# Rebuilding the last stage of an encoder, cross-attention and expert kernel

## The reference, cut to what matters

```python
x1 = x @ sw1.T + sb1;  x2 = x @ sw2.T + sb2
shared_out = ln(silu(x1) * x2, g, b) @ sw3.T + sb3         # all 2048 tokens
x_moe = x[index_b, index_t]                                # 512 chosen tokens
shared_scores = sigmoid(x_moe @ sg_w.T + sg_b)
expert_scores = sigmoid(x_moe @ eg_w.T + eg_b)
top1_idx = argmax(expert_scores + exp_bias)
shared_w, expert_w = softmax([shared_scores, top1_score])
h1 = x_moe @ ew1.T + eb1;  h2 = x_moe @ ew2.T + eb2        # per expert
z = ln(silu(h1) * h2, g', b')
expert_out = (z @ ew3.T + eb3)[top1_idx]
final_out = shared_out.at[index_b, index_t].set(shared_out * shared_w + expert_out * expert_w)
```

## Time and profile before

| | us |
|---|---|
| median of 3 runs | 835.39 (835.33 to 836.73) |
| the profiled execution | 835.16 |
| its span, first to last instruction | 833.4 |
| PE busy | 723.0 (87%) |
| DVE busy | 650.1 (78%) |
| POOL busy | 379.1 (45%) |
| ACT busy | 337.4 (40%) |

### The profile page before, as it was taken

How to read it: one execution, slowest core, us unless ns; L and a number is a source line. 1 busy time by engine, 2 the same in 40 slices (tenths; PEclk the granted TensorE clock), 3 DMA queues, 4 the chain that set the end, 5 groups by cost and what they waited for, 6 DMA issues and landing times.

```text
span 833.4 us, 29134 instructions
## 1 busy us (share of the span) xinstructions
PE 723.0 (87%) x10978; PEld 571.7 (69%) x10978; DVE 650.1 (78%) x1858; ACT 337.4 (40%) x710; POOL 379.1 (45%) x647
## 2 busy tenths in 40 slices
PE   4788469999999999999999999998889888734895
PEld 3567447888888888888888888876556656412673
DVE  4786556787878788887877888789999999845965
ACT  4656224444343444434343444434445545412200
POOL 2788712435353454535444453543345345254132
PEclk9766589999999999999999999999999999955797
DMA  7776300000000000000000000002221222122000
GB/s 272 244 238 226 140 2 2 4 2 4 2 3 3 2 4 3 3 3 3 3 4 3 3 4 9 9 22 73 91 89 60 78 90 80 32 86 75 5 1 6
DMA packets 24655, 41.24 MB, mean 49 GB/s; under 512 B 3727, under 2 KB 16665, under 8 KB 24267
## 3 DMA queue, kind: packets, MB, share of 16 engines
q1 hardware_dynamic: 23096, 37.39, 13.6%
q0 software_dynamic: 704, 1.71, 0.8%
q10 hardware_dynamic: 726, 0.30, 0.1%
HBM read 30.86 MB, written 8.91 MB: 48 GB/s over the span
## 4 chain that ended last, share of the span: by engine, by line
PE 69%; DVE 17%; POOL 5%; issue 5%; ACT 4%; DMA 1%; POOLq 0%; ACTq 0%; DVEq 0%; SPq 0%
PE ps L480 7%; PE ps L474 7%; PE ps L482 6%; PE ps L481 6%; PE ps L684 6%; PE ps L666 5%; DVE mx L1403 5%; PE ps L616 4%; PE ps L722 3%; PE ps L724 3%; PE ps L723 3%; PE ps L618 3%; PE ps L617 3%; PE ps L608 2%; POOL w_lo L1826 2%
## 5 line engine op out<-in xcount | busy, mean ns | idle before, releaser
L1040 ACT ACTIVATE pT<-ps 128x1024 f32<-128x1024 f32 x96 | 93.1, 1022 | 124.5 <-PE ps L666 124.5
L1799 POOL TENSOR_TENSOR rs<-mv,cst 128x1 f32<-128x1 f32 x132 | 31.2, 236 | 178.6 <-DVE mv L1174 140.9
L1403 DVE TENSOR_REDUCE mx<-ps 128x16 f32<-128x2048 f32 x48 | 109.4, 2280 | 1.0 <-PE ps L639 1.0
L1887 POOL TENSOR_TENSOR y<-y,vec 128x256 f32<-128x256 f32 x32 | 23.2, 726 | 170.7 <-DVE y L1177 170.7
L722 PE MATMUL ps<-xh,w_hi 128*128 128x128 bf16 x512 | 99.4, 219 | 0.0
L723 PE MATMUL ps<-xl,w_hi 128*128 128x128 bf16 x512 | 99.3, 219 | 0.0
L724 PE MATMUL ps<-xh,w_lo 128*128 128x128 bf16 x512 | 99.3, 219 | 0.0
L1801 POOL TENSOR_TENSOR rs<-rs,cst 128x1 f32<-128x1 f32 x132 | 73.2, 554 | 10.3
L480 PE MATMUL ps<-w_hi,hh 128*128 x256 | 69.8, 273 | 0.0
L481 PE MATMUL ps<-w_hi,hl 128*128 x256 | 69.8, 273 | 0.0
L482 PE MATMUL ps<-w_lo,hh 128*128 x256 | 69.8, 273 | 0.0
(11 more groups left out here) (366 smaller groups left out, 2495.1 us busy)
## 6 DMA issues: line engine op xcount, KB each, us to landing
stage<-in_w SPq DMA_DIRECT2D x32, 384.0 KB, 3.7
vec<-in_vec SPq DMA_DIRECT2D x4, 896.0 KB, 5.8
vec<-in_tw SPq DMA_DIRECT2D x12, 256.0 KB, 2.8
ctxc<-in_ctx SPq DMA_DIRECT2D x19, 128.0 KB, 2.2
comb<-x SPq DMA_DIRECT2D x16, 128.0 KB, 1.7
comb<-t SPq DMA_DIRECT2D x16, 128.0 KB, 1.8
shared<-x1b SPq DMA_DIRECT2D x16, 128.0 KB, 1.7
out<-x SPq DMA_DIRECT2D x16, 128.0 KB, 1.8
```

The lines of the kernel that those rows point to most:

```text
L1040: A(pT[:, 8 * a:8 * a + 8, :].rearrange("p h q -> p (h q)"), ps[:, 2 * a:2 * a + 2, :].rearrange("p g k -> p (g k)"), ACT.Exp, scale=SCALE ...
L1403: nc.vector.tensor_reduce(mx[:, :], att.rearrange("p g s k -> p (g s) k"), AX.X, ALU.max, negate=True).then_inc(m_max, 1)
```

## The change

The index arithmetic of DVE (`token_rows`) runs once, before DVE's first unit. The keys along the free axis aren't computed any more: PE multiplies each tile's key column, broadcast over 128 columns, by the identity in fp32, so that a PSUM bank holds all 512 keys on every partition; DVE scans that bank four times right after its block 17. PE, ACT and DVE leave their block loops after b = B + 1; what blocks 18 and 19 held of the shared layer stands between steps of the last stage. POOL's gather of the tokens moves from its block 16 to its block 18; the gathers of the shared output are issued two and two behind the second and the third tile's gamma and beta. The expert layers' steps have a new order, with PSUM banks and buffers of their own. Both silus use tanh: x (1 + tanh(x/2)) / 2, in one fused DVE operation, the half being taken up in the gate product.

```diff
@@ sync
-            sp.dma_start(row_i[:, 0, :], ibr_d.broadcast_to([128, M])).then_inc(row_in, 16)
-            sp.dma_start(row_i[:, 1, :], itr_d.broadcast_to([128, M])).then_inc(row_in, 16)
...
+                if b == B:
+                    sp.wait_ge(oT_psum, UNITS + B)
+                    sp.dma_start(tb, tb_d).then_inc(tb_in, 16)
                 put_shared(b - 4)
...
-            sp.wait_ge(oT_psum, UNITS + B)
-            sp.dma_start(tb, tb_d).then_inc(tb_in, 16)
@@ tensor
-            for b in range(1, B + 4):
+            for b in range(1, B + 2):
                 block_c(b, b % 2, ex_of(UNITS - 1)[0] if b == 1 else None)
-            pe.wait_ge(tw_lo, TCHUNKS)
-            pe.wait_ge(tw_hi, TCHUNKS)
+
+            pe.wait_ge(d_gidx, 1)
+            pe.wait_ge(pT_b, UNITS + B)
+            for t in range(MT):
+                last = mm(ps[:, 0, 128 * t:128 * t + 128], ids[:, 4, t:t + 1].broadcast_to([128, 128]), ident,
+                          start=True, stop=True)
+            last.then_inc(d_keys, 1)
...
+            sh_out(B - 2, B - 1)
             pe.wait_ge(tg_split, 1)
...
+            sh_z(B - 1)
             pe.wait_ge(d_sel, D1)
...
-            for step, t in ((choice, 0), (choice, 1), (chosen_hidden, 0), (choice, 2), (chosen_hidden, 1), (choice, 3),
-                            (chosen_z, 0), (chosen_hidden, 2), (chosen_out, 0), (chosen_z, 1), (chosen_hidden, 3),
-                            (chosen_out, 1), (chosen_z, 2), (chosen_out, 2), (chosen_z, 3), (chosen_out, 3)):
+            choice(0)
+            choice(1)
+            chosen_hidden(0)
+            sh_out(B - 1, B - 1)
+            for step, t in ((choice, 2), (chosen_hidden, 1), (choice, 3), (chosen_hidden, 2), (chosen_z, 0),
+                            (chosen_hidden, 3), (chosen_z, 1), (chosen_out, 0), (chosen_z, 2), (chosen_out, 1),
+                            (chosen_z, 3), (chosen_out, 2), (chosen_out, 3)):
                 step(t)
@@ scalar
-                A(sde[:, 0:HM], h[:, 0:HM], ACT.Exp, scale=-1.0).then_inc(s_e, 1)
+                A(sde[:, 0:HM], h[:, 0:HM], ACT.Tanh, scale=0.5).then_inc(s_e, 1)
...
+            sh_zhi(B - 1)
             act.wait_ge(d_oT, D1)
@@ vector
-                ts(sde[:, HM:2 * HM], sde[:, 0:HM], 1.0, None, ALU.add).then_inc(s_e1, 1)
-                dve.wait_ge(s_e1, b + A1)
-                nc.vector.reciprocal(sde[:, 0:HM], sde[:, HM:2 * HM]).then_inc(s_r, 1)
-                dve.wait_ge(s_r, b + A1)
-                tt(h[:, 2 * HM:3 * HM], h[:, 0:HM], sde[:, 0:HM], ALU.mult).then_inc(s_a, 1)
+                stt(h[:, 2 * HM:3 * HM], sde[:, 0:HM], 1.0, h[:, 0:HM], ALU.add, ALU.mult).then_inc(s_a, 1)
...
+            token_rows()
             dve.wait_ge(g_words, 1)
             words_dve.append(word_of(dve, 0))
...
+            for b in range(1, B + 2):
                 block_c(b, b % 2)
+
+            dve.wait_ge(row_in, 16)
+            dve.wait_ge(d_keys, 2)
+            for t in range(MT):
+                last_of_equal(t)
...
+            sh_gnorm(B - 1)
+            sh_sum(B - 2)
...
+            sh_zlow(B - 1)
...
+            mask_tokens(0)
+            mask_tokens(1)
+            sh_sum(B - 1)
+            stored_rows()
+            for step_of, t in ((mask_tokens, 2), (gated, 0), (gated_norm, 0), (mask_tokens, 3), (gated, 1), (mask_z, 0),
+                               (gated_norm, 1), (gated, 2), (mask_z, 1), (gated_norm, 2), (gated, 3), (mask_z, 2),
+                               (gated_norm, 3), (final, 0), (mask_z, 3), (final, 1), (final, 2), (final, 3)):
                 step_of(t)
@@ gpsimd
-                block_c(b, b % 2, ..., gather_tokens if b == B else None)
-            pool.wait_ge(s_shared, 16 * (B + 1))
-            gather(2 * D, 3 * D, shared_d, d_gshared)
+                block_c(b, b % 2, ..., gather_tokens if b == B + 2 else None)
...
+                if t in (1, 2):
+                    pool.wait_ge(s_shared, 16 * (B + 1))
+                    gather(2 * D, 3 * D, shared_d, d_gshared, (2 * t - 2, 2 * t - 1))
```

More of the change, by code:

```diff
@@ L125, in encoder_kernel @@
 def encoder_kernel(nc, x_d, ctx_d, mask_d, maskt_d, w_d, wc_d, vec_d, vc_d, b1_d, gw_d, gb_d, sw_d, sv_d, tw_d, tvec_d, tg_d, tb_d,
-                   ib_d, it_d, ibr_d, itr_d, cst_d, kst_d, pos_d, out, comb_d, shared_d):
+                   ib_d, it_d, cst_d, kst_d, pos_d, out, comb_d, shared_d):
     f32, bf16, i32 = mybir.dt.float32, mybir.dt.bfloat16, mybir.dt.int32
@@ L225, in encoder_kernel @@
         comb = vec[:, R_COMB:R_COMB + MT * 3 * D]
-        rows = w_lo[:, W_ALL - 16 * M:].bitcast(f32).rearrange("p (k m) -> p k m", m=M)
-        row_i, row_f, pos = rows[:, 0:2, :].bitcast(i32), rows[:, 2:4, :], rows[:, 4, :]
-        row_tmp, row_flat, row_key = rows[:, 5, :], rows[:, 6, :], rows[:, 7, :]
+        rows = w_lo[:, W_ALL - 4 * M:].bitcast(f32).rearrange("p (k m) -> p k m", m=M)
+        pos, row_tmp = rows[:, 0, :], rows[:, 1, :]
         finD = vec[:, R_FIN:R_FIN + MT * D]
@@ L289, in encoder_kernel @@
             l2_stats, y2_ready, x_acc)
+        d_keys = g_prod
         A1, D1 = B + 1, UNITS + 1
@@ L893, in _ @@
             pe.wait_ge(tb_in, 16)
+            pe.wait_ge(tw_lo, TCHUNKS)
+            pe.wait_ge(tw_hi, TCHUNKS)
             def choice(t):
@@ L899, in choice @@
                 for e in range(EM):
-                    last = mm(ps[:, 6 + e // 4, 128 * (e % 4):128 * (e % 4) + 128],
+                    last = mm(ps[:, 2 + e // 4, 128 * (e % 4):128 * (e % 4) + 128],
                               identb[0:EM, e:e + 1].broadcast_to([EM, 128]), ohTb[:, 128 * t:128 * t + 128],
@@ L926, in chosen_out @@
                 pe.wait_ge(d_zm, D1 + t)
+                if t == 0:
+                    pe.wait_ge(d_ohb, D1 + MT - 1)
                 if t >= 2:
@@ L1633, in _ @@
             dve.wait_ge(vec_in, 16 * E)
[L1634 to L1644, removed]
             links = [0]
@@ L1673, in rows_of, with token_rows, last_of_equal, stored_rows @@
                 i_link(tt(key, key, flat, ALU.add))
[L1675 to L1679, removed]
+            def token_rows():
+                dve.wait_ge(idx_in, 32)
+                rows_of(idx_i[:, 0, :], idx_i[:, 1, :], ids[:, 0, :], ids[:, 1, :], ids[:, 2, :], ids[:, 3, :], ids[:, 4, :])
+                i_link(cp(gidx[:, :], ids[:, 3, :]))
+                nc.vector.memset(junk[:, 2:3], 0.0).then_inc(d_gidx, 1)
+            def last_of_equal(t):
+                i_link(stt(row_tmp, ps[:, 0, :], ids[:, 4, t:t + 1], pos, ALU.is_equal, ALU.mult))
+                i_link(nc.vector.tensor_reduce(ids[:, 5, t:t + 1], row_tmp, AX.X, ALU.max))
+            def stored_rows():
+                i_link(tt(ids[:, 6, :], ids[:, 5, :], cst[:, C_M:C_M + MT], ALU.is_gt))
+                i_link(ts(ids[:, 7, :], ids[:, 6, :], float(4 * B * S), None, ALU.mult))
+                i_link(tt(ids[:, 8, :], ids[:, 7, :], ids[:, 4, :], ALU.add))
+                i_link(cp(sidx[:, :], ids[:, 8, :]))
+                nc.vector.memset(junk[:, 0:1], 0.0).then_inc(d_sidx, 1)
+            token_rows()
+            dve.wait_ge(g_words, 1)
+            words_dve.append(word_of(dve, 0))
+            for n in range(-1, UNITS + 1):
+                if n == UNITS - 1:
+                    dve.wait_ge(vc_in, 16)
+                block(n, n % 2, vc[:, VC_V:VC_V + D] if causal(n + 1) else bias_of(n + 1), (n - 4) // 2, stats_of(n + 3),
+                      norm_of(n + 2))
+            y_of(at(3), B + 3, UNITS)
+            dve.wait_ge(sv_in, 32)
+            for b in range(1, B + 2):
                 block_c(b, b % 2)
+            dve.wait_ge(row_in, 16)
+            dve.wait_ge(d_keys, 2)
+            for t in range(MT):
+                last_of_equal(t)
             dve.wait_ge(tvec_in, 16)
@@ L1733, in gated @@
                 dve.wait_ge(d_e, D1 + t)
[L1734 to L1738, removed]
+                link(stt(hD[:, 0:HM], de[:, HM * (t % 2):HM * (t % 2) + HM], 1.0, h12[:, 0:HM], ALU.add, ALU.mult))
+                link(stt(hD[:, 2 * HM:3 * HM], hD[:, 0:HM], 0.5, h12[:, HM:2 * HM], ALU.mult, ALU.mult))
+                link(nc.vector.bn_stats(st[:, 2, :], hD[:, 2 * HM:3 * HM]))
                 nc.vector.bn_aggr(mv[:, 2, :], st[:, 2, :]).then_inc(d_var, 1)
@@ L1753, in final @@
             def final(t):
-                shared = (t2, acc)[t % 2]
+                shared = (t2, sum_odd)[t % 2]
                 if t == 0:
@@ L1959, in _, with gather @@
             y_root(B + 3)
-            def gather(c0, c1, rows_d, done):
-                for t in range(MT):
+            def gather(c0, c1, rows_d, done, tiles=range(MT)):
+                for t in tiles:
                     nc.gpsimd.indirect_dma_start(out=comb[:, t * 3 * D + c0:t * 3 * D + c1], out_offset=None,
```

21 lines of the change are left out of this document (13 added, 8 removed).

## The result

The changed kernel took 837.25 us (median, 836.77 to 839.42) against 835.62 before in the same runs: ratio 1.0022, 95% interval 1.0012 to 1.0032. It is slightly slower; forecast was 821.3. The profiled execution took 837.31 us, its span is 835.5.

A forecast was written before the change was run, and what follows sets the result against it. Attention blocks up to 724 us were taken as a ring of PE and DVE, then one chain of small steps over four engines. -6.8 - 7.9 - 1.35 + 2.2 = -13.85 from 835.16 gave 821.3 us, range 815.5 to 828.5.

The forecast's parts named there:

- Part 1: Shared layer's silu by tanh: about 1.1 us less DVE work a block turns idle; value 0, bounds 0 and 16.
- Rival (C): Attention blocks: shorter silu saves 1.1 us in each of 11 blocks, 12 less, 809 us; chance 0.07.
- Part 2: Index arithmetic moved to DVE's start: costs 2.2 us there (bounds 0.6 and 4.3), wins 1.2 in the tail.
- Part 3: Token gathers behind the last shared pieces: first choice product 6.8 us earlier, the 1.2 of Part 2 included.
- Part 4: Expert layers: PE stays fed over the hidden products, output products have half the matmuls, one new wait; -7.9 us.
- Part 5: Scatters at the end: only one issue and its landing, 2.95 us, remain after the last sum; -1.35 us.
- Rival (A): ACT tables: tanh outside exp's set, two loads per shared piece and hidden product; +36, 857 us; chance 0.05.
- Rival (B): Last stage late again: delayed gathers, dearer start, output products at 1.2 GHz, a buffer wait; 828.4 us; chance 0.20.
- (D): No slow clock at the end and a start of +0.6: 817.7 us; chance counted within the forecast's 0.66.

The follow-up runs named there:

- e2: Changed kernel with the index arithmetic back ahead of DVE's block 15: 833.6 us, ratio 0.9970 to the kernel before.
- e10: Kernel before with only the index arithmetic moved to DVE's start: 840.8 us, ratio 1.0049 to the kernel before.
- e8: e6 with the index arithmetic behind DVE's first unit and the token gathers back in POOL's block 16: 821.7 us, against 814.6 with the gathers late.
- e4: Kernel before with only the shared layer's silu by tanh in one fused operation: 849.7 us, ratio 1.0162 to the kernel before.
- e6: Changed kernel with DVE's gate product behind the maxima, their split and the low part of the output: 821.6 us, ratio 0.9834 to the kernel before.
- e5: Changed kernel with POOL's weight subtraction moved ahead of the bias and the sum: 823.5 us, ratio 0.9856 to the kernel before.

## Why the prediction was wrong

**Part 1, silu, is the step that failed.** "The saved time turns into idle" was right: the value bias starts when PE lets it. But I took from that a value of 0 with the bounds 0 and 16 of gain, and excluded a loss without giving a reason; measured was a loss of 13.8. The working looked only at who waits for the silu on DVE. It did not follow what stands behind the silu in DVE's queue: the normalization of the batch ahead, for which POOL's gamma and beta wait, and behind these in POOL's queue the root, the bias, the sum and the weight subtraction, all earlier now. Both facts needed were in the profile before. The gate product started 0.17 us ahead of the subtraction, and in the last two blocks, where the order was the other way, the same line took 1 us:

```profile
705.42 1.16 POOL L1911 TENSOR_TENSOR w_lo<-vec,w_hi 128x512 bf16<-128x512 f32 x1
...
705.73 1.00 DVE L1561 TENSOR_TENSOR h<-h 128x128 f32<-128x128 f32 x1
...
706.65 2.28 DVE L1403 TENSOR_REDUCE mx<-ps 128x16 f32<-128x2048 f32 x1
```

The summary of that line gives the warning in one row (shortest, median, longest in ns):

```profile
L1561 DVE TENSOR_TENSOR h<-h x16: 279/364/997, 572.3 to 755.1; 128x128 f32<-128x128 f32 x16
```

A longest of 997 beside a median of 364 says that there is a neighbour. Nine blocks at 0.65 and five spells of slow clock, 1.4 to 1.6 each, made the loss, about as large as the whole forecast gain. Rival (C) had the sign wrong as well: shorter blocks were the only other outcome that I priced.

**Part 2, the start, was mis-sized**: +2.2, upper bound 4.3, measured +5.8. The timeline of DVE after, at the end of the slow operations, with POOL's two lines that run beside them:

```profile
96.69 5.11 POOL L1862 TENSOR_TENSOR stage<-pT,stage 128x256 bf16<-128x256 f32 x8 [5.84 <-DVE chosen L1371]
...
99.37 0.58 DVE L1661 CAST ids<-idx_i 128x4 f32<-128x4 int32 x1
...
103.65 0.72 POOL L1881 TENSOR_TENSOR ybo<-y,vec 128x256 f32<-128x256 f32 x1
...
103.75 0.65 DVE L1666 TENSOR_SCALAR ids<-ids 128x4 f32<-128x4 f32 x1
...
104.43 0.16 DVE L1667 TENSOR_TENSOR ids<-ids 128x4 f32<-128x4 f32 x1
...
107.97 0.42 DVE L1410 TENSOR_TENSOR v<-ps,vec 128x256 f32<-128x256 f32 x1 [1.04 <-issue]
```

I let only tensor_tensor operations wait for POOL. Here casts and operations of one tensor wait as well: all of the first eight take 0.58 to 0.65 instead of 0.16 to 0.17, about one of POOL's own (5.11 us for eight, 0.64 each). That is 8 x 0.43 = 3.4 where I took 1. With the word loads behind the work (1.04 where I had 1.2) the first maxima are 4.8 later, counted from the gate arithmetic. The next three units add 1.5 (40.78 us from maxima 0 to 3 against 39.31), at a granted clock of 0.81 instead of 0.90 between 100 and 155 us; that I had no term for. It comes with the early index work: the five kernels that have it take 40.8 to 41.1, the seven others 39.1 to 39.8. Of the 1.2 counted as won back in the tail, e2 and e10 show 0.3 and 0.4.

The Trainium skill (SBUF — State Buffer, Who interferes with whom) says that copies, casts and tensor_scalar can enter modes in which they too lock GpSimd out or are locked out, and that the order of issue decides who blocks. The trace agrees, with 0.58 for a cast of 128x4 and with 0.36 against 0.99 for the gate product. I had quoted only its sentence on two SBUF inputs.

**Part 3 was right.** -8.0 against -6.8, and e8 shows 6.3 in the tail for the gathers' place alone. The gathers landed as the scans ended.

**Part 4 was right.** -8.8 against -7.9. PE was nearly gapless over the hidden products; the wait at the third output product came, but as two, 1.73 for the last gamma and beta and 1.19 for a final sum, and its clock fell behind them as forecast.

**Part 5**: -0.7 instead of -1.35. Issue and landing of the last scatter take what was counted (2.8 us from its start to the span's end), but it starts 0.8 behind the last sum, for which nothing was counted.

**Rival (A)** is refuted: ACT loads one table, as before. Rival (B), a late last stage, is refuted too: of its places only the start lost time, 3.6 more than forecast where (B) had 2.1. The slow clock at the end came, so (D) had that part wrong.

The chance of 0.05 for "slower" rested on the table load alone. With the gate product's row read, both signs had to be open for part 1.

## What to carry to other kernels

Making an operation shorter can move what stands behind it on every engine, also where the time saved is idle: follow what stands behind it, and who waits for that, to the next pair of DVE and POOL operations that read SBUF, and ask which of the two starts first. A line whose longest instance is far above its median has such a neighbour; if it stands right ahead of what PE waits for, put it behind that. Small operations moved into a "free" gap paid one POOL operation each here beside a row of POOL's two-input operations, so count POOL's row, not DVE's idle time.

## What was not expected of the hardware

- Tiny DVE operations (128x4, also cast and tensor_scalar) took 0.58 to 0.65 us each beside a row of POOL tensor_tensor operations of 0.64, and 0.16 to 0.17 without it. Reductions and a reciprocal of the gate arithmetic, of 128x16 results, took 0.22 to 0.25 beside the same row.
- The order decides who pays: 0.17 us ahead of POOL's subtraction the gate product took 0.36 us, 0.31 us behind it 0.99. The maxima, read from PSUM, took 2.28 to 2.29 in either case.
- With a regular wait of 2.11 to 2.16 us ahead of the shift's transpose in each block, TensorE stood at 1.2 GHz behind every second one only from unit 39 on; in e2 and e4 two such blocks also follow one another (14.38 and 14.23; 14.38 and 14.25). With waits of 1.46 (e6) and 1.70 (e5) it stayed at 2.4 GHz. What decides in which of them it falls stays open.
